# Four pairs of constant TensorE products in the second batch's attention of a decoder layer

## What is computed

```python
x = x + attention(layernorm(x))      # 16 heads of 16, in two chunks of 128 positions
x = x + cross(layernorm(x), ctx)     # softmax over a normed similarity with 64 context features
x = x + experts(layernorm(x))        # 8 experts of 256x256, the best 2 of each row weighted

# attention, for each head and chunk of 128, with a carried state kv
inter  = (q_i * q_decay) @ kv
scores = (q_i @ k_i.T) * dmask
out    = inter + scores @ v_i
kv     = r_C * kv + (k_i * k_decay).T @ v_i
# then attn = rms_norm(out) @ Wo

# experts
logits = h @ Wr                      # top 2 of 8, softmax of the two
out    = sum_e gate_e * (h @ We[e] + be[e])
```

## Time and profile before

| | |
|---|---|
| median of three timed runs | 149.0 us |
| lowest and highest | 147.78 and 150.75 us |
| the profiled execution | 148.25 us |
| its span, first to last instruction | 145.9 us |
| mean granted clock of PE over the span | 0.96 |
| PE busy | 130.7 us, 90% |
| PE weight loads busy | 98.0 us, 67% |
| DVE busy | 101.3 us, 69% |
| ACT busy | 72.8 us, 50% |
| POOL busy | 31.6 us, 22% |

### The profile page before, as it was taken

The page is one execution under the profiler, slowest core; times in us unless marked ns, Lnnn a source line. Parts: engine busy times, 40 slices in busy tenths (PEclk is TensorE's granted clock), DMA queues, the critical chain, the costliest instruction groups (busy, mean ns, idle before and its releaser), DMA issues.

```text
span 145.9 us, 3109 instructions
## 1 busy us (share of the span) xinstructions
PE 130.7 (90%) x1063; PEld 98.0 (67%) x1063; DVE 101.3 (69%) x330; ACT 72.8 (50%) x228; POOL 31.6 (22%) x58
## 2 busy tenths in 40 slices
PE   0799989999866999999998999999999997699990
PEld 0455677886544797876777887767787676487870
DVE  0454899459797761764998659799846849879553
ACT  4278648979897015578437639440143453411300
POOL 7125400630820200102262040103002113020110
PEclk9999999999997558999999999999999999999998
DMA  3999980000000000000000002000002000002002
GB/s 117 286 363 315 351 228 2 7 0 4 0 0 0 4 0 4 0 0 0 0 2 7 0 4 72 0 0 2 4 0 74 4 0 0 0 6 66 0 0 72
DMA packets 7934, 7.29 MB, mean 50 GB/s; under 512 B 2264, under 2 KB 7792, under 8 KB 7792
## 3 DMA queue, kind: packets, MB, share of 16 engines
q1 hardware_dynamic: 7424, 6.79, 14.7%
q10 hardware_dynamic: 496, 0.32, 0.8%
HBM read 6.06 MB, written 1.05 MB: 49 GB/s over the span
## 4 chain that ended last, share of the span: by engine, by line
PE 58%; DVE 11%; SPq 9%; ACT 6%; issue 6%; DMA 4%; POOL 3%; DVEq 1%; ACTq 0%; POOLq 0%
PE ebank L1104 25%; PE chain L1234 5%; DMA xin<-in_x 4%; PE chain L1104 4%; PE front L1104 4%; PE chain L1259 4%; PE chain L1219 3%; PE front L1309 2%; DVE acc L977 2%; PE front L1096 2%; DVE zg L893 2%; SPq L314 2%; DVE probs L861 2%; PE chain L1248 2%; DVE zb L897 1%
## 5 line engine op out<-in xcount | busy, mean ns | idle before, releaser
L1104 PE MATMUL ebank<-w_e_hi,h3T_hi 128*128 128x512 f32 x56 | 20.0, 438 | 2.3 <-DVE acc L977 1.5
L861 DVE TENSOR_TENSOR probs<-chain,dec 128x512 f32<-128x512 f32 x32 | 19.9, 679 | 0.0
L977 DVE SCALAR_TENSOR_TENSOR acc<-ebank,gate_y,acc 128x256 f32<-128x256 f32 x40 | 17.4, 476 | 3.4 <-PE ebank L1104 3.2
L1104 PE MATMUL ebank<-w_e_hi,h3T_lo 128*128 128x512 f32 x56 | 18.0, 403 | 0.0
L1104 PE MATMUL ebank<-w_e_lo,h3T_hi 128*128 128x512 f32 x56 | 18.0, 403 | 0.0
L1104 PEld LDWEIGHTS ebank<-w_e_hi,h3T_hi 128*128 128x128 f32 x56 | 9.2, 193 | 6.1 <-DVE acc L977 3.1
L1104 PEld LDWEIGHTS ebank<-w_e_lo,h3T_hi 128*128 128x128 f32 x56 | 10.8, 193 | 2.6
L1104 PEld LDWEIGHTS ebank<-w_e_hi,h3T_lo 128*128 128x128 f32 x56 | 10.8, 193 | 2.6
L1219 PE MATMUL chain<-qx,kT 32*128 32x256 f32 x128 | 9.4, 405 | 2.3 <-DVE probs L861 1.8
L358 POOL TENSOR_TENSOR rot_b<-qk,cst 128x128 f32<-128x128 f32 x16 | 7.6, 495 | 17.2 <-ACT qk L492 17.2
L1234 PE MATMUL chain<-probs,vpad 128*32 128x128 f32 x256 | 9.5, 311 | 0.5 <-issue 0.5
(11 more groups left out here) (180 smaller groups left out, 294.4 us busy)
## 6 DMA issues: line engine op xcount, KB each, us to landing
w_e<-in_L_ffn_We SPq DMA_DIRECT2D x2, 1024.0 KB, 9.1
xin<-in_x SPq DMA_DIRECT2D x4, 256.0 KB, 5.1
dec<-in_decay SPq DMA_DIRECT2D x1, 1024.0 KB, 6.7
out<-outb SPq DMA_DIRECT2D x8, 128.0 KB, 1.8
w_qkv<-in_L_attn_Wq SPq DMA_DIRECT2D x1, 256.0 KB, 4.2
w_qkv<-in_L_attn_Wk SPq DMA_DIRECT2D x1, 256.0 KB, 4.6
w_qkv<-in_L_attn_Wv SPq DMA_DIRECT2D x1, 256.0 KB, 4.8
w_o<-in_L_attn_Wo SPq DMA_DIRECT2D x1, 256.0 KB, 6.9
```

The source lines that it names most:

```text
L861: nc.vector.tensor_tensor(probs[:, t, r], chain[:, r], dec[:, r], ALU.mult).then_inc(s_sc, 1)
L977: nc.vector.scalar_tensor_tensor(out=outb[:, t, :] if last else acc[:, t, :], in0=expert_bank(b, q, t)[:, (e % 2) * D:(e % 2 + 1) * D], sc ...
L1104: mm = pe.matmul(dst, a[ka][:, c, a_cols], b[kb][:, c, b_cols], start=(n == 0 and c == 0), stop=(n == 2 and c == KC - 1))
```

## The change

A new helper, keep_warm, makes two constant products of 256 columns to ebank1. Ahead of them it waits for the same three counters that guard ebank in expert(0,0,0). It is called four times in PE's list.

```diff
+            def keep_warm():
+
+                pe.wait_ge(s_state, 2)
+                pe.wait_ge(s_qkT, TILES * 2)
+                pe.wait_ge(s_qd, 2)
+                for _ in range(2):
+                    keep_clock(ebank[1], 256)
+
...
             transpose_qk(2,0)
             transpose_qk(2,1)
+            keep_warm()
             states(2)
+            keep_warm()
             scores(1,1)
+            keep_warm()
             transpose_x2(0,0)
             transpose_x2(0,1)
+            keep_warm()
             expert(0,0,0)
             logits(0)
             attend(1)
```

## The result

| | before | changed |
|---|---|---|
| timed runs, median | 149.58 us (4 runs, 147.78 to 150.75) | 152.16 us (4 runs, 151.95 to 153.25) |
| profiled execution | 148.25 us, span 145.9 | 151.95 us, span 149.8 |
| mean granted clock | 0.960 | 0.989 |

The ratio is 1.027, 95% interval 1.016 to 1.038. The changed kernel is slower, by 1.8 to 2.7% (whether by more than 2% these runs don't settle), though its clock is higher on average. The forecast was 149.6 us and "within 2%".

What follows compares the result with a forecast made beforehand. PE was taken as the bound, the end of attend(1) moving the kernel's end. Onto 148.25 us: start +0.75, pairs +4.30, states +0.30, scores -0.27, transpose -0.41, cast to attend -1.68, attend -1.66, together +1.33: 149.6 us, range 147.6 to 151.6.

Steps and rivals of the forecast that it cites:

- The base of the sum: Whole execution: differences were added to the profiled 148.25 us, without the 0.75 us to the timed runs' median.
- The wait: Ahead of pair one: PE waits for DVE's masked states, without work from 42.32 to 45.50, 3.2 us.
- The fall: At the idle time ahead of pair one: PE's clock falls to half, at about the same place as now.
- The length of the low stretch: From pair one on: 3.7 us of half clock from 45.50, full clock from 49.2.
- case C: Low stretch from pair one of 5.5 us: 0.47 us per further microsecond, so 150.5; chance 0.65 together with the forecast.
- The price of a pair: Each keep_warm call on PE: 0.86 us at full clock, 1.72 at half, taken from projecting attention.
- Pair four was hidden: Behind the second x2 transpose: the fourth pair runs while DVE's work still holds back attend(1), costing nothing.
- DVE bounded attend: At attend(1): its start belongs to DVE's decayed scores, 3.55 + 0.14 us behind ACT's cast; PE idle 0.2 to 0.6 us.
- Rival A: Clock never falls in the middle: attend(1) ends at 55.91, execution 147.85 us, within 2%; chance 0.19.
- 4.5 us more: Kernel before, scores to attend(1): extra time from half clock, about the most the change could win back, less its price.
- Slower by over 2%: Whole execution: chance 0.11 that the changed kernel is more than 2% slower.
- rival B: Clock falls and stays low to 55.80: attend(1) ends at 60.2, 3.9 us later, execution 152.15 us; chance 0.11.

Runs made afterwards that it cites:

- before_again: The kernel before, with no edit, measured and profiled once more: 150.35 us median (10 runs) beside 150.38, ratio 0.9955.
- after_again: The changed kernel, with no further edit, measured and profiled once more: 152.31 us median (4 runs), ratio 1.0175.
- after_warm_start: The changed kernel plus three products of a zeroed tile ahead of PE's first wait: 151.07 us median (4 runs).
- after_clock_held: The changed kernel plus six constant products in PE's idle time ahead of pair one: 150.22 us median beside 150.82 for the kernel before.
- before_warm_start: The kernel before plus three products of a zeroed tile ahead of PE's first wait: 146.89 us median beside 149.17 unedited.
- wait_only: The changed kernel without its products: only keep_warm's three waits ahead of states(2), other three calls gone; 151.79 us median beside 149.17 for the kernel before.

## Why the prediction was wrong

The measured median, 152.16, lies 0.6 us over the range, and 2.6 over the forecast. Going by the steps:

- **The base of the sum is the step that failed.** The sum was made on the 148.25 us of the profiled execution, and the 0.75 us to the median was left off with the reason that if the spread comes from the low stretch, "that stretch is what the sum replaces". The reason was half right. The low stretch does differ between executions of the kernel before (mean clocks 0.960 to 0.988), but the start does too, and nothing in the sum replaces that: 39.91 against 42.80 for the same program. The profile of before had a short start. The sum put the difference at the start at nothing; it is 2.14 us of the 3.9 between the two profiled spans, and most of the 2.6 by which the forecast missed. The rows of the start were in view and were used only as a price. That before_again shows the late start without the change makes it a matter of the execution; what decides it stays open.
- **The wait was right.** Pair one was put at 45.50, which is +5.59 from scores(1,0); it came at +5.55, with 3.12 us of idle ahead of it against the 3.2 foreseen.
- **The fall was right**, and "about the same place": 47.58, within 0.1 us of pair one, as in the sum. In after_again and after_warm_start it came 0.5 to 0.7 us ahead of pair one, still in the hole.
- **The length of the low stretch was half right.** 3.7 us were taken; it was 3.4 in two profiles and 6.8 in two. For the latter, case C stops at 5.5 us, with 0.85 us more; its own 0.47 for each microsecond gives 1.5 more at 6.8, and the profiles show 1.3 (19.42 against 18.11). The price was right and the length beyond the case.
- **The price of a pair was too small.** 0.86 us at full clock and 1.72 at half, from the earlier trace rows; the runs show 0.96 to 1.06 and about 2.0 to the next work. From pair one to ACT's cast the sum has 5.93 us and the trace 6.38 (53.98 - 47.60). With attend 3.65 us behind the cast for 3.69 and pair one 0.04 earlier, this is the whole of 1.70 against 1.33. Why a pair takes longer here than the two products of the projection was not tested.
- **Pair four was hidden and DVE bounded attend**, as the sum has it. PE is idle for 0.25 us ahead of attend, 0.2 to 0.6 foreseen. The chain calls this "issue" and names no releaser; DVE's last decayed scores end at 57.54 (56.26 + 1.28), 0.09 ahead of attend:

```profile
56.26 1.28 DVE L861 TENSOR_TENSOR probs<-chain,dec 128x512 f32<-128x512 f32 x2
```

- **Rival A had the right price, nearly**: after_clock_held is 16.58 for the sum's 16.00 (55.91 - 39.91). The difference is again the pairs.
- **A sum that is off without effect.** The "4.5 us more" of low clock comes to 4.15 by the terms named there (1.50, 0.71, 1.66 and 0.28); the trace without a fall gives 3.83. The forecast does not use it.
- **The chances failed at the edge.** "Slower by over 2%" held 0.11 and only rival B, a long low stretch. The real way there was a small local loss on a base that was itself too low; that B's 152.15 is also the measured median is a coincidence, since its low stretch to 55.8 did not happen. The interval of the ratio, 1.016 to 1.038, and those of the two repetitions lie around that limit.

## What to carry to other kernels

Here constant products kept the clock where they ran in the hole, in 20 runs of 20. A product that waits for a later event than the real work behind it (the masking at +5.55, when states(2) had run at +3.22 and the scores at +4.84) leaves the hole open, and holds that work back. So choose its bank by when its last reader is through, not by which bank is used next. And before summing on one profiled execution, compare its time to the timed runs and find, ahead of the changed place, what can differ between executions: a base that is 2 us low is a larger error than most terms of such a sum.

## What the runs showed of the hardware

- The start of this kernel differs by 2.9 us between executions of one program (scores(1,0) at 39.91 and 42.80), through PE's half rate in its first work lasting to about 8 us or to about 14. The granted clock reads 1.00 there all the same; only the durations show it (1.22 against 0.70 us for one product). Three products of zeros from 2.04 us on, ahead of the first real work, went with the short start in four profiles of four.
- The same idle pattern on PE, 0.81 and 1.28 us with a third of a microsecond of narrow products between, brought a fall to half clock in two profiles (before, before_again) and none in a third (before_warm_start).
- PE came back to full clock after 3.4 or 6.8 us in the four profiles of the changed kernel (with either start), after 6.8 us in wait_only, which has no constant products in this place, and after 10.2 us in both profiles of the kernel before. Of the 47 runs of the kernel before, eleven have a higher mean clock than these two profiles (0.975 or 0.988 for 0.960 and 0.963). So the length differs between executions of one program, and how much of it the work behind the fall decides is not shown.
